# The fifteen middle rounds of a two-layer attention and mixture kernel: a hardware loop with register waits becomes straight code with constant waits

## What is computed

```python
x = L0_attn_x                                   # (16, 512, 128)
xn = _layernorm(x, axis=-1)
s = _L0_attn_ref(xn, ...)                       # 4 small transformer layers, see below
g = _silu(_L0_ffn_ref(xn, ...))                 # 8 experts of width 256, the best 2 of each token
x = x + s * g
xn = _layernorm(x, axis=-1)
s = _L1_attn_ref(xn, W_qkv, W_out)              # 16 heads of 64, windows of 128 tokens, one window back
g = _silu(_L1_ffn_ref(xn, ...))                 # 32 experts of width 64, the best 4, and a shared one
x = x + s * g
```

## Time and profile before

| | |
|---|---|
| median of 3 runs | 4673.15 us (4673.07 to 4688.22) |
| the profiled execution | 4671.39 us |
| its span in the profile | 4669.6 us |
| TensorE's granted clock, mean over the span | 0.956 of full |
| instructions in the trace | 75535 |

### The profile page before, as it was taken

The page is one execution under the profiler, slowest core; times in us unless marked ns, Lnnn a source line. Parts: engine busy times, 40 slices in busy tenths (PEclk is TensorE's granted clock), DMA queues, the critical chain, the costliest instruction groups (busy, mean ns, idle before and its releaser), DMA issues.

```text
span 4669.6 us, 75535 instructions
## 1 busy us (share of the span) xinstructions
PE 4215.7 (90%) x20080; PEld 2591.7 (56%) x20208; DVE 3738.3 (80%) x8946; ACT 3231.8 (69%) x6125; POOL 2055.7 (44%) x2033
## 2 busy tenths in 40 slices
PE   5669999898998989999898998989999898999979
PEld 3336556565565656555565665656556565655655
DVE  4779798787978879798787978879798887979843
ACT  2447777676776767777676777767777676777745
POOL 1235455444444444454444534544444444445523
PEclk8779999999999999999999999999999999999979
DMA  4011111011111111111111111101111111111100
GB/s 130 14 28 27 30 32 35 26 31 32 29 27 32 35 27 32 29 30 32 29 31 33 27 27 33 36 23 31 33 30 28 31 33 30 27 29 32 35 21 21
DMA packets 144533, 149.42 MB, mean 32 GB/s; under 512 B 27748, under 2 KB 107932, under 8 KB 143960
## 3 DMA queue, kind: packets, MB, share of 16 engines
q1 hardware_dynamic: 144088, 144.19, 11.9%
HBM read 22.45 MB, written 4.19 MB: 6 GB/s over the span
## 4 chain that ended last, share of the span: by engine, by line
PE 40%; DVE 22%; issue 21%; POOL 8%; ACT 6%; SPq 1%; DVEq 1%; DMA 0%; POOLq 0%; ACTq 0%
DVE acc L952 5%; PE bT L1326 5%; PE bU L1364 5%; DVE tmp L952 4%; PE bA L1174 4%; PE bG L1357 4%; PE bC L1371 4%; PE bA L1264 3%; PE bT L1158 3%; POOL s_h L644 3%; DVE nmax L1100 3%; PE bA L1255 2%; PE bT L1284 2%; DVE hu L1139 2%; PE bT L1339 2%
## 5 line engine op out<-in xcount | busy, mean ns | idle before, releaser
L644 POOL TENSOR_TENSOR s_h<-s_h,ge 128x512 f32<-128x512 f32 x512 | 712.6, 1392 | 1184.1 <-ACT ge L654 954.4
L952 DVE TENSOR_TENSOR tmp<-comps 128x512 f32<-128x512 f32 x768 | 585.1, 768 | 8.9
L1371 PE MATMUL bC<-hu,w_d 128*128 128x512 f32 x1056 | 572.3, 624 | 8.7 <-DVE hu L1139 8.2
L776 ACT ACTIVATE s_h<-bG 128x512 f32<-128x512 f32 x528 | 314.8, 596 | 376.9 <-PE bG L1357 208.5
L952 DVE TENSOR_TENSOR acc<-acc,tmp 128x512 f32<-128x512 f32 x768 | 567.3, 740 | 8.0
L753 ACT ACTIVATE probs<-bT,nmax 128x256 f32<-128x256 f32 x1024 | 408.1, 474 | 185.9 <-DVE nmax L1100 183.5
L1139 DVE TENSOR_TENSOR hu<-bU,s_h 128x512 f32<-128x512 f32 x528 | 362.3, 686 | 173.9 <-POOL s_h L644 103.8
L631 POOL TENSOR_TENSOR rot<-rot,sinT 128x512 f32<-128x512 f32 x256 | 355.2, 1388 | 303.5 <-DMA rot<-raw 303.5
L1326 PEld LDWEIGHTS bT<-V,probsT 128*128 128x128 f32 x3584 | 430.8, 193 | 80.6 <-issue 37.1
L622 POOL TENSOR_TENSOR comps<-comps 128x255 f32<-128x255 f32 (+1 forms) x384 | 298.0, 776 | 379.5 <-ACT comps L700 379.4
L1326 PE MATMUL bT<-V,probsT 128*128 128x65 f32 x3584 | 442.0, 276 | 13.4 <-ACT probsT L654 12.2
(11 more groups left out here) (201 smaller groups left out, 9392.8 us busy)
## 6 DMA issues: line engine op xcount, KB each, us to landing
rot<-raw SPq DMA_DIRECT2D x1024, 64.0 KB, 2.0
comps<-comps SPq DMA_DIRECT2D x384, 120.0 KB
x_ld<-in_L_attn_x SPq DMA_DIRECT2D x66, 128.0 KB, 2.2
comps<-comps SPq DMA_DIRECT2D x384, 8.0 KB
out<-O SPq DMA_DIRECT2D x16, 256.0 KB, 2.9
w_a<-in_L_attn_W_qkv SPq DMA_DIRECT2D x1, 1536.0 KB, 14.5
w_fc<-in_L_attn_fc_w SPq DMA_DIRECT2D x1, 1024.0 KB, 7.9
w_g<-in_L_ffn_w_gate SPq DMA_DIRECT2D x1, 1024.0 KB, 6.0
```

The source lines that it names most:

```text
L644: nc.gpsimd.tensor_tensor(s_h[:, :], s_h[:, :], ge[:, :], ALU.mult).then_inc(weighed, 1)
L776: nc.scalar.activation(s_h[:, :], bG[:, :], ACT.Silu).then_inc(silu, 1)
L952: V_.tensor_tensor(dst, i0, i1, op).then_inc(ham[h], 1)
L1371: ins = mm(bC[:, :], down, hu[:, :], start=u in (0, UNITS0), stop=u in (UNITS0 - 1, UNITS - 1))
```

## The change

The loop of the five engines becomes a Python loop. Nothing else is touched:

```diff
         def rounds(eng, one):
 
             one(first)
-            with eng.Fori(1, NB) as i:
+            for i in range(1, NB):
                 one(middle(i))
             one(last)
```

## The result

| | before | changed |
|---|---|---|
| median (range), 4 runs each | 4675.48 us (4673.07 to 4688.22) | 4645.49 us (4641.74 to 4647.94) |
| span of the profiled execution | 4669.6 us | 4643.4 us |
| TensorE's granted clock, mean | 0.956 | 0.962 |
| mean distance of two borders in the middle rounds (last L1084 to last L1084) | 278.03 us | 276.42 us |

The ratio is 0.993, with a 95% interval of 0.9916 to 0.9944: faster by 0.7%. The forecast was 1.0% (4628 us), and the range to 4648 us held the result with little to spare. What the prediction said of the border's length came true; the borders alone are worth more than the whole gain.

What follows compares the result with a forecast made beforehand. Bound: the chain through DVE's stall at each round border, with PE near its limit. Sum: 4671.4 - 38.4 (back edges) - 0 (registers) - 7 (clock) = 4626.0 us, given as 4628 us for the runs' median; range 4602 to 4648 us.

Steps and rivals of the forecast that it cites:

- the border's length: Between two rounds, from L1084 to the transpose on PE: 3.00 us instead of 5.74 us.
- The back edges, 38.4 us: At fourteen round borders, DVE's stall behind its branch back goes, shortening the chain by 2.74 us each: 38.4 us less.
- Rivals 1 and 2: At the border, 1: POOL or PE work decides, 4654 us, 5%; 2: a branch costs only itself, 4672 us, 2%.
- PE's stall brings nothing of its own: At the border, removing PE's stall of 2.06 us gains nothing, as the transpose still waits for DVE.
- The register operations, 0: In the loop body, they run while the instruction ahead computes; removing them brings 0, bounds 0 to 0.2 us a round.
- The clock, 7 us at the borders: Behind the borders, half of the drops to half clock vanish: 0.5 us a round, 7 us in all.
- The extra stretches in mid round, left at six,: Half-clock stretches in mid round stay in six rounds; none would be 8 us less, one in each 11 us more.
- The code, 0 us: Instruction fetch: straight code needs the same bytes less the register operations', and fetching ahead costs nothing.
- Rival 3, slower by late code,: In straight code, DVE's instruction blocks arrive late, 2.7 us each; at two a round 4711 us; chance 4%.

Runs made afterwards that it cites:

- start 0: DVE alone straight, PE's loop moved to begin at instruction 0 of a block of 256, against the kernel before: 4631.13 us, ratio 0.9906.

## Why the prediction was right, and where not

- *The back edges, 38.4 us.* Right in mechanism, place and size. The border shrank from 5.66 to 5.95 us to 2.92 us, which is 14 x 2.8 = 39 us. Rivals 1 and 2 fall with it: nothing else holds the border, and the 2.84 us behind the branch were the branch's, as they come back where DVE alone loops (2.80 us). The Trainium skill (Advanced Engine Details and Errata, Control Flow Timing) gives about 108 ns for a compare-and-branch; DVE's took 63 ns, and the 2.84 us behind it are some 26 times that figure.
- *PE's stall brings nothing of its own.* Nearly right: eleven of fifteen borders are 3.0 us long with PE's branch in place. In four PE's branch was late and cost 0.1 to 1.4 us.
- *The register operations, 0.* Right: with them left in, 4648.62 us against 4645.49, intervals nearly the same. What they do cost is the 0.08 us a round at the border, 1.1 us in all.
- *The clock, 7 us at the borders.* The size was right (0.6 us a round against 0.5), the way was not: not half of the borders escaped but one of fourteen, and the others had a stretch of 3.4 us (once 6.8) instead of 6.8 (three times 10.2). With PE alone in the loop half did escape, seven of fourteen. *The extra stretches in mid round, left at six,* became nine. At 1.4 us each, the term's own price, that is 4 us. The best ends of all terms add up to 4598 us while the range began at 4602; the result lies near the other end.
- *The code, 0 us.* **This is the step that failed.** The prediction counted bytes and asked whether straight code reaches DVE in time. It does; no issue wait appeared. It didn't ask what a fetch does to others, nor what keeps the fetches in place. The loop did: PE's packets came at the same points of every round, points at which the order of SP's DMAs had been harmless. Written out, PE's code of 10.2 packets a round drifts against the round, and its packets meet SP's issues where DVE waits for them, at up to 0.9 us a hit. What straight code cost in place of the 0 us: 12.5 us where DVE kept its loop (4689.9 against 4677.42), and at one clock 13 to 15 us in the changed kernel, measured against those with the same border and fetches out of the way. The result missed the forecast by 17 us. Of the 13 to 15 us, hits that the traces locate make 5 to 10; the rest is shown by the kernels' times alone. The kernels with DVE straight and PE's fetches out of the way have ratios of 0.9899 to 0.9912 (start 0, with hits and a higher clock, has 0.9906 too), where the forecast was 4628 / 4673.15 = 0.9903.
- *Rival 3, slower by late code,* named the right resource, instruction fetches, but not the engine that loses by them. The Trainium skill (Runtime: NRT & Kernel Launch, Instruction fetch mechanics) calls crossing a block mostly hidden; for the engine whose code it is the traces agree, with no issue wait on DVE in straight code. SP, which starts DMAs at that moment, is held: 0.59 us became up to 1.8 in the changed kernel.
- *The end.* From the last border to the end it takes 197.33 us instead of 200.07, 2.7 us less. That isn't the change's: the second trace of the same kernel has 201.06 us, so these 2.7 us of the profiled execution's 26 are scatter.

## What to carry to other kernels

Ask of a loop's back edge which engine's stall lies on the chain between rounds; only that one need be unrolled, and the others' loops may stay. Unrolling an engine with much code can take its instruction fetches out of step with the round, as it did PE's here, and a fetch can delay a DMA issue by a microsecond, so look at what stands in the issuing queue behind long groups of issues, and put what is needed first ahead. When two versions differ by less than the spread that the granted clock makes, compare them round by round, with the same pattern of clock, before deciding that a change did nothing.

## What was unexpected of the hardware

- A fetch of 16 KB of PE's code that begins within a microsecond of the start of a DMA issue of SP lengthens it, in one case of three, from 0.59 us to 1.0 to 2.1 us.
- The cost of a branch back is not the branch: 0.06 us on DVE, then 2.8 us without code; with a prefetch hint 0.4 us.
- Moving only the start of PE's loop within a block of 256 instructions changed the program by 28 us (4631.18 to 4658.99 us).
- A spread by the clock nearly as wide as the gain of the change: six runs of one kernel had mean granted clocks of 0.959 to 0.967 and times of 4649 to 4622 us, 27 us apart.
